# Waits on column transforms ahead of the load pairs of SyncE in a four-layer spectral kernel

## What is computed

```python
x = _L0_conv_ref(x, w1, b1, w2, b2)    # rfft2, relu, softshrink, irfft2, + input
x = _L1_conv_ref(x, ...)               # layer norm, rfft2, gelu, irfft2, + input, then the MLP:
m = _ln(h, ln2_g, ln2_b)
m = _gelu(m @ mlp_w1 + mlp_b1) @ mlp_w2 + mlp_b2
return m + residual
x = _L2_conv_ref(x, ...)               # as the first layer, with its own weights
x = _L3_conv_ref(x, ...)               # as the first layer, with its own weights
```

## Time and profile before

| | |
|---|---|
| median of 3 runs | 2064.04 us |
| the three runs | 2058.64, 2064.04, 2066.43 us |
| span of the profiled execution | 2057.0 us |
| PE busy | 1919.2 us, 93% of the span |
| DVE, ACT, POOL busy | 57%, 49%, 21% |
| moved by DMA | 141.05 MB, mean 69 GB/s |
| DMAs of 384 KB that load a unit: issue to landing | 8.8 us (median) |
| DMAs of 384 KB that store a unit: issue to landing | 5.4 us (median) |

### The profile page before, as it was taken

One profiled execution on the slowest core, in us unless ns is written; L12 is line 12 of the kernel. 1 busy time (PEld: TensorE's weight loads), 2 busy tenths in 40 slices (PEclk: granted clock), 3 DMA queues, 4 the chain that ended last, 5 costly groups with the idle time before them and its releaser, 6 DMA issues.

```text
span 2057.0 us, 68971 instructions
## 1 busy us (share of the span) xinstructions
PE 1919.2 (93%) x31104; PEld 1570.9 (76%) x31104; DVE 1173.7 (57%) x2480; ACT 1008.7 (49%) x1644; POOL 435.4 (21%) x425
## 2 busy tenths in 40 slices
PE   4999995698998999999999999999899999999996
PEld 3777772576776999999999999999777777777774
DVE  3687887977855433333333333332377767677675
ACT  3766545576753333333333333333466666665652
POOL 3212104965631000000000000000221211221200
PEclk9999997799999999999999999999999999999998
DMA  9425738307434111111111111114532573557314
GB/s 164 100 49 85 129 62 142 55 4 129 114 86 122 32 31 31 31 31 31 31 31 31 31 31 31 31 31 73 94 53 49 87 127 80 84 99 126 60 40 96
DMA packets 299701, 141.05 MB, mean 69 GB/s; under 512 B 275760, under 2 KB 298032, under 8 KB 299440
## 3 DMA queue, kind: packets, MB, share of 16 engines
q1 hardware_dynamic: 299440, 137.08, 36.2%
HBM read 74.14 MB, written 62.91 MB: 67 GB/s over the span
## 4 chain that ended last, share of the span: by engine, by line
PE 80%; DVE 9%; SPq 3%; ACT 2%; issue 2%; POOL 2%; DMA 1%; DVEq 0%; POOLq 0%; ACTq 0%
PE ps L693 20%; PE ps L678 19%; PE ps L586 8%; PE ps L523 8%; PE ps L537 7%; PE ps L602 6%; PE ps L555 5%; PE ps L504 4%; DVE u L937 3%; DVE st L974 2%; SPq L357 1%; DVE xs L962 1%; PE ps L565 1%; DMA wraw<-in_w 1%; PE ps L663 1%
## 5 line engine op out<-in xcount | busy, mean ns | idle before, releaser
L1086 DVE TENSOR_TENSOR gl<-g,gh 128x512 fp32r<-128x512 f32 x192 | 156.8, 816 | 476.3 <-ACT gh L872 476.3
L937 DVE TENSOR_TENSOR u<-ps,clamp 64x192 f32<-64x192 f32 (+1 forms) x864 | 378.1, 438 | 27.7
L869 ACT ACTIVATE g<-ps,colp 128x512 f32<-128x512 f32 x192 | 132.3, 689 | 529.1 <-PE ps L678 529.1
L523 PEld LDWEIGHTS ps<-const,z 128*48 128x48 f32 x8384 | 266.0, 124 | 134.9 <-issue 128.6
L732 ACT ACTIVATE z<-ps 64x512 f32<-64x512 f32 x366 | 234.9, 642 | 155.1 <-PE ps L504 148.2
L523 PE MATMUL ps<-const,z 128*48 128x64 f32 (+1 forms) x8384 | 270.3, 217 | 10.2 <-issue 5.3
L1173 POOL COPY xn<-xs 128x512 f32<-128x512 f32 x144 | 152.0, 1096 | 535.8 <-PE ps L504 343.9
L693 PE MATMUL ps<-w2h,gh 128*128 128x384 f32 x768 | 261.9, 341 | 0.0
L693 PE MATMUL ps<-w2h,gl 128*128 128x384 f32 x768 | 258.6, 337 | 0.0
L693 PE MATMUL ps<-w2l,gh 128*128 128x384 f32 x768 | 257.5, 335 | 0.0
L586 PEld LDWEIGHTS ps<-const,u 128*64 128x64 f32 x6144 | 206.7, 139 | 52.2 <-issue 25.7
(11 more groups left out here) (70 smaller groups left out, 2463.4 us busy)
## 6 DMA issues: line engine op xcount, KB each, us to landing
after<-xs SPq DMA_DIRECT2D x96, 384.0 KB, 5.4
xs<-after SPq DMA_DIRECT2D x94, 384.0 KB, 8.8
after<-om SPq DMA_DIRECT2D x32, 384.0 KB, 4.3
out<-xs SPq DMA_DIRECT2D x32, 384.0 KB, 5.5
xm<-after SPq DMA_DIRECT2D x30, 384.0 KB, 6.3
xs<-in_x SPq DMA_DIRECT2D x24, 384.0 KB, 8.4
wstage<-in_spectral SPq DMA_DIRECT2D x16, 210.0 KB, 5.8
xs<-in_x SPq DMA_DIRECT2D x4, 768.0 KB, 11.9
```

What stands on the lines that cost most here:

```text
L523: mm = pe.matmul(ps[a * SIDE:a * SIDE + BLOCK, F2_BANK, n * L.kh:(n + 1) * L.kh], z[:, g % 2, slot, :], basis(col + a * SIDE, L.kh), start ...
L937: dve.tensor_tensor(u[to, g % 2, :, start + b:start + size:BATCH], whole, limited, ALU.subtract).then_inc(u_ready, 1)
L1086: dve.tensor_tensor(gl[:, n % 4, :], g[:, n % 2, :], gh[:, n % 4, :], ALU.subtract).then_inc(g_low, 1)
```

## The change

SP waits for `f2_done` ahead of each pair of a unit's load. `load_slots(unit)` gives the four slots for the load of unit+3: slots 0 to 3 of group 2 unit + 4 where that group's layer has 9 slots, slots 0 to 3 of group 9 for unit 3, and none for units 2 and 4 (the loads of units 5 and 7), nor in the MLP's loop for unit 8. The loads of units 1 and 2 wait for slots 1 to 4 and 5 to 8 of group 0, those of units 9 and 10 for slots 0 to 3 of groups 16 and 17. No DMA is added, removed or reordered, and the other engines' lists are the same.

```diff
+def load_slots(unit):
+
+    g = 2 * unit + 4
+    if unit == PAIRS - 1:
+        return [(g - 1, n) for n in range(PARTS)]
+    return [(g, n) for n in range(PARTS)] if layer_of(g).full else None
...
-            def load_unit(unit):
+            def slot_begun(g, t):
+                sp.wait_ge(f2_done, groups_before(g) + t + 1)
+
+            def load_unit(unit, at=None):
                 for part in range(PARTS):
+                    if at:
+                        slot_begun(*at[part])
                     for b in range(BATCH):
                         load_rows(unit, b, part)
...
-                        load_unit(unit + 3)
+                        load_unit(unit + 3, load_slots(unit))
...
-            load_unit(1)
+            load_unit(1, [(0, 1 + n) for n in range(PARTS)])
             load_weights(1)
-            load_unit(2)
+            load_unit(2, [(0, 1 + PARTS + n) for n in range(PARTS)])
...
-            load_unit(2 * PAIRS + 1)
-            load_unit(2 * PAIRS + 2)
+            load_unit(2 * PAIRS + 1, [(2 * BLOCKS, n) for n in range(PARTS)])
+            load_unit(2 * PAIRS + 2, [(2 * BLOCKS + 1, n) for n in range(PARTS)])
```

## The result

The change is slower: median 2073.12 us of 7 runs (2070.29 to 2076.76) against 2062.23 us of 7 runs of the kernel before (2054.46 to 2066.43). The ratio is 1.0054, 95% interval 1.0035 to 1.0073, so 7 to 15 us, 10.9 by the medians. I had forecast no change, with 2055 to 2073 as range.

A forecast was written before the change was run, and what follows sets the result against it. The prediction took PE to bound the kernel, with SP's queue the path in the head. Terms +7.5 - 3.9 - 2.0 - 1.4 = +0.2 us, carried to the median, gave 2064 us, range 2055 to 2073.

The forecast's parts named there:

- So in the head SP's queue is the path: Head, loads of units 1 and 2: waits delay SP's queue and `wraw` behind it, through to PE's end; +7.5 us.
- Unit 1 is late as well: 0: Head, group 2's first row transform: half a microsecond late from unit 1, hidden by the wait for `wraw`; 0 us.
- Unit 6, all, -1.4: Layer 1: moving unit 6's load to group 9 takes away all of the 1.45 us stall at its old place; -1.4 us.
- Units 9 and 10, -2.0: Right after the MLP: 16 loads go out in two pieces with a gap, removing half of 3.9 us; -2.0 us.
- I take half: -3.9: Units 3, 4 and 11 to 15: a queue half as deep removes half of 7.8 us of stalls; -3.9 us.
- rival A: Loads of units 3, 4, 9 to 15: engines as full as before, stalls stay; +6.1 us, 2070 us, chance 0.27.
- Rival D: Head, ACT's `wraw` copy in group 1: full 11.2 us queue shift plus 2.4 us slower clock; 2076 us, chance 0.11.

The follow-up runs named there:

- e1_head_only: The change with only the waits of units 1 and 2 kept, later loads issued as in the kernel before: ratio 1.0054 against the kernel before.
- e11_change_copies_later: The change with ACT's copies of `wraw` moved from group 1 to slots 1 to 6 of group 2: ratio 1.0007 against the kernel before.
- e4_wide: Kernel before with pairs of units 3, 4 and 9 to 15 behind slots 0, 2, 4 and 6: ratio 0.9971.
- e8_singles_all: Kernel before with units 3, 4 and 9 to 15 loaded by paced single DMAs, first `wraw` load ahead of unit 2: 2047.32 us, ratio 0.9906.
- e2_all_but_head: The change with units 1 and 2 loaded as before, all other waits kept: ratio 1.0013 against the kernel before.
- tiny loads: Kernel before with loads of units 3, 4, 6 and 11 to 15 bringing 1 row instead of 16 a DMA: ratio 0.9917.
- e6_unit6_late: Kernel before with only the load of unit 6 moved behind slots 0 to 3 of group 9: ratio 1.0025.

## Why the prediction was wrong

- **"So in the head SP's queue is the path": right.** Term +7.5; measured 7.7 us at the first store in the change, 7.9 by the means of the heads. `e1_head_only` has 9.9 in its profile and 11 (8 to 14) by its ratio, so the term may be too small by a few us; where they would arise is open. The reading behind it, `wraw` ahead of ACT's ordered list ahead of PE, is shown by `e11_change_copies_later`. The first copy of `wraw`, forecast for 73 to 74, came at 72.52, the idle stretches of 8 to 9 us as stated. SP's last load of unit 2 went out from 61.75 on, where I had said 63; slot 1 was reached 3 us earlier than in the earlier trace rows, so the load of unit 1 began at 32.96, not 36.4. In two other kernels with this head it began at 35.47 and 36.32; this much varies from run to run.
- **"Unit 1 is late as well: 0": right.** PE waited 0.4 us for POOL's turn, ahead of the 8.35 us. In `e1_head_only` it was 2.5 us, ahead of 8.09 us.
- **"Unit 6, all, -1.4": wrong in sign; one of the two steps that failed.** I put the stall of the earlier trace rows down to the load that stands beside it in time. It stays without any load, 1.44 us against 1.45. I should have seen that it follows 12 us of waiting, right at the beginning of a segment. And the load, moved to group 9, makes a stall there whose price is the slower clock behind it: +2.6 us by the means of the profiles.
- **"Units 9 and 10, -2.0": wrong in sign; the other step.** I took half of their stalls as gone because the loads come in two pieces. From the MLP's last store to the first of layer 2 the four kernels with these pairs take 110.3 to 112.1 us, the eight with the burst of before 107.9 to 110.9: +2.0 us by the means, and 1.9 in the change's own profile. Pairs in every second slot (`e4_wide`) take 113.4 us, single DMAs (`e8_singles_all`) 106.7. Why pairs are worse than the burst here, and better in layers 2 and 3, is open.
- **"I take half: -3.9" for units 3, 4 and 11 to 15: right in size, as far as the profiles tell.** Units 11 to 15 give 3.9 us by the means of the table above, units 3 and 4 about 1 (from the first to the fourth store 202.0 us against 203.0). That the number was this close is luck: my reason, one pair queued instead of two halves the stalls, holds only roughly (4.3 to 6.5 us against 6.3 to 10.5), and the first profile, from which I had the stalls, was short of them.
- **The sum.** Head +7.9, units 3, 4 and 11 to 15 -4.9, unit 6 +2.6, units 9 and 10 +2.0: +7.6 us by the profiles, at the low end of the 7 to 15 by the ratio. The forecast of +0.2 had 7.3 us for gains behind the head. `e2_all_but_head`, which has all waits but the head's, is not faster but 3 us slower (1 us faster to 7 slower). The mechanism of the loss was right. The range ended 0.1 us below the median.
- **The rule of the Trainium skill** ("DMA: Bandwidth & Descriptors", queues, rings and completion order: turns between queues by packet) gave rival A, 2070 us. A's time is 3 us off, D's 2076 as well, and neither is right by its reasons: units 3, 4 and 11 to 15 did give something, and `wraw` landed well before 76 us. The reason that I drew from the rule, that the number of queued loads would not matter, is refuted by 5.3 against 0.3 us at equal traffic.
- **Rival D** described the place and the slower clock rightly, and its estimate of 2.4 us is what the three slow groups lost. Not all of it reached the end: ACT's first two copies of `wraw` are 6.4 us later than before, the third to the last 7.6 to 7.8, so at most 1.2 us went through. The late load of 11 us did not occur.
- **The baseline.** I counted 13.1 us of stalls from one execution that was quick because it had few of them; the ceiling with tiny loads is 17 us for fewer units. The full stretch of the earlier trace rows has PE busy for 17.76 of 18 us, so it was weak evidence for stalls in the first place.

## What to carry to other kernels

When loads disturb the engine that bounds the kernel, pace them in single transfers with room between, not in bundles: against bursts, bundles of two gave 4 us in layers 2 and 3, or 6 with twice the room, singles with room 11. Look first at what stands behind such waits in the same queue: here it was a load that an ordered list waits for at once, and that cost more than the pacing gave. Small stalls that differ from run to run are taken from several profiles, not one; and remove their supposed cause in one run, as with the tiny loads, before sizing what a cure may bring. A stall that stands beside a load in time need not come from it. And a short stall can cost more than its length when the clock falls behind it.

## What the runs showed of the hardware

- Instructions come by the DMA engines too (queue q8 on the page of the change: 224 packets, 3.67 MB, so 16 KB each). Data loads beside them make stalls of PE: 6.3 to 10.5 us between 1600 and 1940 us with bursts, none with the tiny loads. That the link is a late instruction block is an inference. The Trainium skill, "Runtime: NRT & Kernel Launch", section on instruction fetch mechanics, names blocks of 16 KiB, which agrees, and calls the cost of crossing one mostly hidden. If the stalls are such crossings, single ones are not: in layers 2 and 3 they reach 2.8 us in the second profile of before.
- Stalls come back at the same places of PE's list. In the kernel before a row transform is interrupted ahead of its last 20 matmuls at 1497.89 us (1.35 us); the same 20 are held up in the change (1505.14, 1.35 us) and in `e4_wide` (1498.38, 1.62 us), but not in `e8_singles_all`: the list decides where a stall can be, the loads whether and how long. Not every stall hangs on loads: the one ahead of layer 1's row transforms is 1.44 us in `e6_unit6_late` with a DMA share of 0.00.
- Two idle times of PE close together, 1.43 and 0.70 us with 1.15 us of work between, were followed by a granted clock of 0.51 (`e6_unit6_late`); one of 1.62 us at the same place was not (before).
- The time for one kernel spreads over 12 us between runs (2054.46 to 2066.43), which is as much as the effect of this change.
